# Where the first attention's output is turned and divided: in the attention, or in the projection that reads it

## What is computed

```python
x = x + attn1(group_norm(x)) @ proj_w + proj_b      # 12 heads of 16, 1024 tokens an image
t = tokens(x)
t = t + attn2(layer_norm(t))                        # own Wq, Wk, Wv, no projection behind
t = t + experts(layer_norm(t))                      # one expert of 16 for each token
```

## Time and profile before

| | |
|---|---|
| median of 3 runs | 3111.39 us (3110.06 to 3124.24) |
| the profiled execution | 3100.89 us, its span 3099.0 us |
| TensorE busy | 2711.8 us (88%) |
| VectorE busy | 2344.3 us (76%) |
| ScalarE busy | 1938.1 us (63%) |
| POOL busy | 909.4 us (29%) |
| granted TensorE clock, mean | 0.926 |

### The profile page before, as it was taken

The page is one execution under the profiler, slowest core; times in us unless marked ns, Lnnn a source line. Parts: engine busy times, 40 slices in busy tenths (PEclk is TensorE's granted clock), DMA queues, the critical chain, the costliest instruction groups (busy, mean ns, idle before and its releaser), DMA issues. The chain is left out here.

```text
span 3099.0 us, 57198 instructions
## 1 busy us (share of the span) xinstructions
PE 2711.8 (88%) x20914; PEld 1057.6 (34%) x20914; DVE 2344.3 (76%) x3662; ACT 1938.1 (63%) x3195; POOL 909.4 (29%) x1426
## 2 busy tenths in 40 slices
PE   5887899999999999997799599999999999981787
PEld 3765122222222222221565222222222222270565
DVE  4554799999999999993363699999999999671222
ACT  2443167766766676676344299999999999920333
POOL 0011333333333333321323111111111111045776
PEclk9777599999999999999899699999999999975899
DMA  5777555445445545533466331111111111160221
GB/s 114 216 228 219 106 104 112 102 101 112 102 98 112 105 100 105 110 85 64 117 196 180 109 94 50 50 49 49 50 49 48 48 48 48 50 153 1 59 63 45
DMA packets 210601, 298.41 MB, mean 96 GB/s; under 512 B 59596, under 2 KB 146326, under 8 KB 205746
## 3 DMA queue, kind: packets, MB, share of 16 engines
q0 software_dynamic: 67200, 170.53, 23.5%
q1 hardware_dynamic: 143156, 124.61, 14.9%
HBM read 186.25 MB, written 109.19 MB: 95 GB/s over the span
## 5 line engine op out<-in xcount | busy, mean ns | idle before, releaser
L458 ACT ACTIVATE a_probs<-a_psS 128x1024 f32<-128x1024 f32 x768 | 744.2, 1021 | 381.4 <-PE a_psS L371 381.3
L931 DVE TENSOR_REDUCE a_halfmax<-a_psR 128x2 f32<-128x1024 f32 x768 | 885.9, 1218 | 33.3 <-PE a_psR L759 31.5
L880 ACT ACTIVATE a_probs<-a_psS 128x512 f32<-128x512 f32 x1536 | 835.1, 596 | 89.7 <-PE a_psS L775 65.5
L503 DVE TENSOR_REDUCE h_halfmax<-a_psR 128x1 f32<-128x512 f32 x768 | 490.3, 685 | 48.1 <-PE a_psR L353 43.2
L503 DVE TENSOR_REDUCE a_halfmax<-a_psR 128x1 f32<-128x512 f32 x768 | 492.6, 686 | 39.3 <-PE a_psR L353 34.5
L796 PE MATMUL a_psO<-a_probs,a_v 128*32 128x256 f32 x6144 | 491.4, 391 | 21.0 <-ACT a_outT L862 19.7
L371 PE MATMUL a_psS<-a_qrows,a_krows 121*128 121x512 f16 x1536 | 402.1, 383 | 38.5 <-DMA a_qrows<-relh 37.4
L382 PE MATMUL a_psO<-a_probs,a_v 128*32 128x512 f32 x3072 | 410.1, 606 | 0.6 <-ACT a_probs L458 0.6
L796 PEld LDWEIGHTS a_psO<-a_probs,a_v 128*32 128x32 f32 x6144 | 122.4, 108 | 320.6 <-ACT a_probs L880 264.1
L353 PE MATMUL a_psR<-h_kmax,h_qmax 64*128 64x512 f16 x768 | 178.9, 405 | 21.8 <-POOL h_ident L39 21.5
L371 PEld LDWEIGHTS a_psS<-a_qrows,a_krows 121*128 121x128 f16 x1536 | 120.4, 98 | 225.9 <-DMA a_qrows<-relh 58.2
(11 more groups left out here) (211 smaller groups left out, 3202.9 us busy)
## 6 DMA issues: line engine op xcount, KB each, us to landing
qk<-p_half SPq DMA_DIRECT2D x96, 256.0 KB, 3.4
a_qrows<-rel POOLq DMA_DIRECT2D x96, 256.0 KB, 4.2
a_v<-v POOLq DMA_DIRECT2D x96, 256.0 KB, 3.0
v<-p_v SPq DMA_DIRECT2D x36, 512.0 KB, 6.1
a_qrows<-qk POOLq DMA_DIRECT2D x144, 128.0 KB, 4.8
relh<-p_rel SPq DMA_DIRECT2D x48, 256.0 KB
attn<-a_out SPq DMA_DIRECT2D x96, 128.0 KB, 2.2
rel<-p_rel SPq DMA_DIRECT2D x36, 256.0 KB
```

What stands on the lines that cost most here:

```text
L458: nc.scalar.activation(PT[:, blk % 2, 2 * pair:2 * pair + 2, :], psS[:, b0:b0 + 2, :], ACT.Exp, scale=scale).then_inc(exped, 1)
L503: nc.vector.tensor_reduce(mx[:, unit, half:half + 1], psR[:, slot, :], AX.X, ALU.max)\
L880: nc.scalar.activation(PT[:, blk % 2, o, :], psS[:, bank(m), :], ACT.Exp, scale=scale)\
L931: nc.vector.tensor_reduce(MX[:, unit:unit + UNITS // QH // 2 + 1:UNITS // QH // 2, kh], psR[:, slot, :].rearrange("p (r k) -> p r k", r=2) ...
```

## The change

The first attention no longer has back jobs. ScalarE's copy `OT`, channels by queries with the sums, is stored as it is, so `O1` in HBM holds, for each step, 128 rows (per head 16 outputs and 16 sums) of 1024 tokens in place of 64 channels by tokens. ScalarE's copy waits for the store of the same half of the step before. The ring's places go round plainly.

The second projection reads from it, for each round, outputs `O` and sums `SU` as 96 channels by 2 by 2048 tokens, in eight transfers from SyncE's queue instead of six from POOL's; those of round 0 stand ahead of the last two weights, those of round j + 1 behind round j's stores of x2. VectorE takes the reciprocal of the sums and multiplies, in four chunks of 512 tokens (`normalise`). TensorE's projection reads `O` straight; its transposes of the output and ScalarE's copies of them are gone.

```diff
-            after[KT + 2].append(("back", 0, 0))
...
+            def store(s, qh):
+                sp.wait_ge(otc, s * QH + qh + 2)
+                sp.dma_start(OD[s][:, 512 * qh:512 * qh + 512], OT[:, qh, :]).then_inc(stored[qh], 16)
...
             def copy_out(s, qh):
                 act.wait_ge(pvdone, s * PVS + KT * (qh + 1) + 2)
-                if before is not None:
-                    act.wait_ge(ring_free, before + 4)
+                if s > 0:
+                    act.wait_ge(stored[qh], 16 * s)
                 nc.scalar.copy(OT[:, qh, :], psO[:, :]).then_inc(otc, 1)
...
-                    nc.vector.reciprocal(RC[:, :, :], o[:, :, HD:HD + 1]).then_inc(recips, 1)
-                    dve.wait_ge(recips, half + 1)
-                    dve.wait_ge(stored[qh], steps * 16 + (16 * j[1] + 16))
-                    nc.vector.tensor_tensor(OS[:, qh, :, :], o[:, :, 0:HD], RC[:, :, :].to_broadcast([P, 4 * GH, HD]),
-                                            ALU.mult).then_inc(ring_free, 1)
...
+            def load_attn(j):
+                heads = ON.rearrange("(b c h) z d t -> b c z h d t", b=B, c=2)
+                for b in range(2):
+                    for of, dst in ((1, SU), (0, O)):
+                        for c in range(2):
+                            sp.dma_start(dst[:, c, b * L:b * L + L], heads[bass.ds(2 * j + b, 1), c, of]
+                                         .rearrange("b h d t -> (b h) d t")).then_inc(oload[b], 16)
...
+                load_attn(0)
                 sp.dma_start(WP[:], W["proj_w"].rearrange("(c p) n -> p c n", p=CC)).then_inc(wload, 16)
...
+                    if not last:
+                        load_attn(j + 1)
                 for m, half in ((0, 0), (0, 1), (1, 0), (1, 1), (2, 0)):
                     store_half(j, m, half)
...
             def proj(i, j):
-                pe.wait_ge(ots, j * NT + i + 3)
+                if i % 4 == 0:
+                    pe.wait_ge(on, j * 4 + (i // 4 + 1))
                 pe.wait_ge(x2, j * NT + i + 1)
...
+            def normalise(j, chunks):
+                for q in chunks:
+                    at = slice(512 * q, 512 * q + 512)
+                    dve.wait_ge(oload[q // 2], j * 64 + 64)
+                    nc.vector.reciprocal(SU[:, :, at], SU[:, :, at]).then_inc(rcp, 1)
+                for q in chunks:
+                    at = slice(512 * q, 512 * q + 512)
+                    dve.wait_ge(rcp, j * 4 + (q + 1))
+                    nc.vector.tensor_tensor(O[:, :, at], O[:, :, at], SU[:, :, at], ALU.mult).then_inc(on, 1)
...
+                if turned:
+                    normalise(j + 1, (0, 1))
                 if not first:
                     low_half(j, 1)
...
+                if turned:
+                    normalise(j + 1, (2, 3))
                 if not first:
                     low_half(j, NCH - 1)
...
             dve.wait_ge(wload, NW)
+            if not first:
+                for q in range(4):
+                    normalise(0, (q,))
```

More of the change, by code:

```diff
@@ L117, in jobs_of @@
                 after[MAXBLK].insert(2, ("rows",))
-            after[KT + 2].append(("back", 0, 0))
-            if not (first and u == 0):
-                after[2].append(("back", -1, 1))
-            if last and u == 1:
-                after[BLK].append(("back", 0, 1))
             return after
@@ L148, in slot_of @@
             return n % 3
-        def slot_free(n):
-            return n + 2 if n < 2 else n + 1
-        assert N_BODY % 3 == 2
-        SHIFT = (1 - (BASE1 - 1)) % 3
-        def first_slot(m):
-            return (m + SHIFT) % 3
-        def back_number(jobs, u, which, qh):
-            return next(n for js in jobs[u] for n, j in js if j[0] == "back" and j[1] == which and j[2] == qh)
         def rows_number(jobs, u):
@@ L332, in step @@
                 else:
-                    store(s, 1, base, back_number(jobs, u, 0, 1))
+                    store(s, 1)
             for u in range(2):
@@ L342, in _, with job @@
             for qh in range(QH):
-                sp.wait_ge(stored[qh], 16 * STEPS + 16)
+                sp.wait_ge(stored[qh], 16 * STEPS)
         @block.tensor
         def _(pe):
-            def job(jn, j, base, slot, free, buf, halves, rows):
-                pe.wait_ge(ring_free, base + free)
+            def job(jn, j, base, buf, rows):
+                slot = slot_of(base + jn)
+                pe.wait_ge(ring_free, base + jn + 1)
                 if j[0] == "max":
@@ L384, in pv, with step @@
                 mm.then_inc(pvdone, 1)
-            def step(i, u, jobs, base, first, last, slot, free):
+            def step(i, u, jobs, base, first, last):
                 s = 2 * i + u
@@ L400, in some @@
                         for jn, j in part:
-                            job(jn, j, base, slot(jn), free(jn), u, halves, s + 1)
+                            job(jn, j, base, u, s + 1)
                     def last_pv():
@@ L415, in step @@
                     pv(u, BLK - 1, blks, halves)
-                    for jn, j in jobs[u][BLK]:
-                        job(jn, j, base, slot(jn), free(jn), u, halves, s + 1)
             pe.wait_ge(const_done, 2)
@@ L442, in _, with copy_out, step @@
             nc.scalar.sem_inc(otc, 1)
-            def copy_out(s, qh, before):
+            def copy_out(s, qh):
                 act.wait_ge(pvdone, s * PVS + KT * (qh + 1) + 2)
-                if before is not None:
-                    act.wait_ge(ring_free, before + 4)
+                if s > 0:
+                    act.wait_ge(stored[qh], 16 * s)
                 nc.scalar.copy(OT[:, qh, :], psO[:, :]).then_inc(otc, 1)
-            def step(i, u, first, last, before):
+            def step(i, u, first, last):
                 s = 2 * i + u
@@ L496, in _, with job @@
             nc.vector.sem_inc(ring_free, 3)
-            def job(jn, j, base, slot, buf, steps):
+            def job(jn, j, base, buf, steps):
+                slot = slot_of(base + jn)
                 dve.wait_ge(ring_full, base + jn + 1)
@@ L508, in job @@
                         nc.vector.tensor_tensor(MC[:, :], mx[:, :, 0], mx[:, :, 1], ALU.max).then_inc(maxed, 1)
-                elif j[0] == "rows":
+                else:
                     if steps is not None:
@@ L1488, in round_of @@
                 dve.wait_ge(vst, j * 96 + 16)
+                turned = not first and not last
                 for n in range(NT // 2):
```

131 lines of the change are left out of this document (37 added, 94 removed).

## The result

| | before | changed |
|---|---|---|
| median of the runs | 3110.72 us (3105.47 to 3124.24) | 3209.88 us (3196.95 to 3211.45) |
| the profiled execution | 3100.89 us, span 3099.0 | 3211.45 us, span 3209.7 |
| granted TensorE clock, mean | 0.926 | 0.904 |

The ratio is 1.0316, 95% interval 1.0289 to 1.0344: 99 us slower, where 3211 us was forecast.

The account below looks back on a forecast made before the run. TensorE, without holes, bounds the first attention; VectorE sets the second projection's low halves, residual and norm. Terms -30 + 96 + 31 + 1 + 3 - 1 = +100 on 3100.9 give 3201, by the median 3211 us; range 3168 to 3252.

Parts of the forecast that it names:

- The division, +96: Second projection, rounds 0 to 2: four chunks of reciprocal and multiply, 32 us a round, added whole before the first residual add.
- Rival 1: Second projection: reciprocal streams one element a cycle, its 98 ns fixed; 3113 to 3126 us, not slower; chance 0.12.
- Round 0, +31: Second projection's start: 27 us of loads, then 32 us of division, move the first residual add from 1489.96 to 1520.7.
- Rival 4: Second projection's start: round 0's loads run at their fast end, +14 instead of +31; 3194 us; chance 0.06.
- POOL's meeting with the division: Second projection, round 0: VectorE's divisions meet POOL's add of x, 0 to 6.7 us, taken as 1.
- The first attention, -30: First attention: 48 back jobs removed at 0.62 us of TensorE each, 30 us less.
- the slack of two blocks: First attention: two blocks (5.2 us) between a row load and its use, so larger stores were taken to cost 0.
- Rival 2: First attention: the larger stores delay the row loads, 22 us; 3233 us; chance 0.06.
- The clock, +3: Second projection, rounds 0 to 2: TensorE idles some 28 us a round, its granted clock falls, 1 us a round.
- Rival 3: Second projection: TensorE's clock stays at the lower level into each query phase, 3 x 5 us; 3223 us; chance 0.06.
- The range's lower end, 3168: Whole kernel: lower bound of 3168 to 3252 us, with -11 named for the reciprocal and -13 for the loads.
- the 10.5 us that it knew of: Whole kernel: the runs' median, 3111.4 us, lay 10.5 above the profiled execution's 3100.9; added to 3201 to give 3211.

## Why the prediction came out as it did

The forecast of 3211 us was met to 1 us and its mechanism holds; one term was badly sized, and part of the agreement is luck.

**The division, +96: right in kind, 6 us too large.** A reciprocal of 1024 took 6.54 us (taken: 6.8), two in a row 12.95; a multiply 1.15 to 1.22. A round's division was 30.2 instead of 32, three of them 90.5. It lies on the path whole: the rounds grew by 92.4, and taking the reciprocals away brought them back to some 65 us. Rival 1 (one element a cycle, 98 ns fixed) fell: 3.32 us at 512 and 6.54 at 1024 make a slope of 6.3 ns. The prediction's reason for the slope, that no other one-operand instruction had such a surplus, was an argument from one size; the run with half the elements shows it. Of the two rules of the Trainium skill weighed there ("VectorE: DVE Perf Modes"), neither gives the measured size: the repeat count of 8 in the section "Walkthrough: the 8-slice pipeline in each mode" was read as an estimate of 8.5 us, the fixed cost and one cycle an element of the section on the TRN2 errata as one of 1.1; the runs say 6.54.

**Round 0, +31: right, +31.3.** The loads were to take 27 us from the first issue to the last landing, at 3.4 us each; with the two weights behind them they took 26.9 (the first stands in SyncE's queue at 1445.65, the last weight had landed at 1472.5), and 32.3 us of division followed. That they ran one after another at that price was taken over from the rows of another transfer, and that the sum came out so closely is in part luck: by the trace's own landings the first load took 8.4 us and each of the others followed 2.5 us behind the one before. What held them showed only afterwards, in the DMA share of 0.40 for an outermost dimension of 6 and 1.03 for 16. The Trainium skill has this as a rule: "DMA: Bandwidth & Descriptors", section "Why a DMA increments its semaphore by 16 and not by 1", says that a transfer is spread over the largest number of engines, up to 16, that divides the outermost dimension on both sides. By that rule the share would be 6/16 = 0.38, an estimate, and the trace agrees with its 0.40. Rival 4, the loads at their fast end, fell for that reason. POOL's meeting with the division was taken at 1 us and cost 1.4 (2.62 instead of 1.22 at 1486.83).

**The first attention, -30: the term that was mis-sized.** It measured -16.5, or -18.2 from its first scores to its last store (1089.2 before, 1071.0 after). The failed step is "TensorE is the engine without holes, so 48 x 0.62": TensorE was busy 1024 of 1070 us, and the 46 us of holes were not looked at. 37.4 of them were waits for rows of relative positions, once a step, directly ahead of the block with the first back job, so the slack of two blocks between a row load and its use, on which the prediction leaned, was already used up there. That back job covered the next such wait. The 24 jobs of block 2 gave their 15 us, those of block 10 little, as the two runs with the transposes put back show: +14.9 and +3.6. With one profile of before, and 1064.5 to 1073.4 us for the same attention in ten, the saving is known as some 16 to 25 us: 30 is outside. Rival 2, the larger stores delaying the row loads, would have shown the same wait and must be told apart: putting the transposes back in block 10, with the larger stores in place, brought the wait back to 37.6, the 37.4 of before, so the stores aren't the cause.

**The clock, +3: about right in size, for a reason that doesn't hold for the queries.** Over the four rounds the queries and keys took 93.0 us after (23.29, 22.85, 23.80, 23.11) and 89.3 before (20.94, 24.35, 20.94, 23.09); the residual stretches of rounds 1 to 3 were 1 to 2 us longer each, that of round 0 1.5 shorter. Rounds 0 to 2 hold 92.4 - 90.5 = 2 us beyond the division. But TensorE's idle time in the division, which the prediction named, isn't needed to lengthen the queries and keys: they were as long where TensorE worked through most of the division (22.90 to 23.94), and where only multiplies were left of it (22.84 to 23.70). They fell to 20.94 in all four rounds only when the waits between the last turned tiles were filled. Why some rounds kept the upper clock through such waits (0 and 2 of the kernel before, 1 and 3 without the reciprocals, 1 with half of them, 2 with the transposes back) and the others didn't stays open. For the residual stretch the prediction's reason may stand: its head in round 1 of the changed kernel had a granted clock of 0.50 (1594 to 1598 us); no run separates that. Rival 3 (the low clock into every query phase) came true in its mark, all four being above 20.94, by 1.9 to 2.9 us instead of 5 a round; but two rounds of before were so too.

**Why the total fits.** The division was 6 us over and the attention's saving 12 to 14 too large; they stand on opposite sides, but don't cancel: profile to profile the change cost 110.7 where 100 was worked out. The difference is the terms' 7 us and the +3.5 from behind round 3's first residual add. By the medians, though, the change cost 99.2, since the profiled execution of before lay 9.8 under its median and the one after 1.6 above its own. The prediction added the 10.5 us that it knew of. So 3211 owes about 10 us to a spread that had nothing to do with the change. The range's lower end, 3168, doesn't follow from the parts named for it: -11 and -13 from 3211 give 3187. The measured time is well above both.

## What to carry to other kernels

A division that moves from a place where one copy of each sum is divided to one where all 16 are, and into a stretch that its engine sets, costs by the element and by the place. So count the elements of the slow instruction first, and look for a stretch in which the same engine waits anyway. When work is removed from an engine that is busy 96% of the time, read what the other 4% wait for: work that stands just ahead of such a wait can be nearly free, as it was here, and taking it away then gives little. Read small effects by stretch, as the untouched rest of a long program can move by more than they are worth.

## What the runs showed of the hardware

- VectorE's reciprocal in f32 took 0.258 us for 16 elements a partition (out of PSUM), 3.32 for 512 and 6.54 for 1024: 6.2 to 6.3 ns an element. The multiply of two f32 operands took 1.22 us for 1024.
- While POOL added f32 tiles, VectorE's multiply was held (1.22 became 2.62 and 4.74 us), but the reciprocal that ran while the same add began (from 1480.25, with POOL's add from 1481.70 to 1488.37) kept its 6.54.
- One reordering of the partitions, which made the outermost dimension of the source 16 instead of 6 with bytes and row length unchanged, took the DMA share of eight loads from 0.40 to 1.03 and their rate from 145 to 247 GB/s.
- With extra matmuls that nobody reads in TensorE's short waits, the granted clock stayed at 1.00 instead of 0.53 at the head of the queries and keys, and these took 20.94 us in each round instead of 22.84 to 23.70; the three rounds became 3.9 us shorter together, since the residual stretches grew.
